# A planner's price for GpSimd's weighting of head pairs, and a new ring layout for VectorE's pairs, in a fused attention and FP4 feed-forward kernel

## The reference

```
xn   = layernorm(x)
q, k, v = split(xn @ w_attn + b_attn)                # 16 heads of 8 features
scores  = q k^T * 8**-0.5 + mask                      # mask = -log(delta + 1) for a key delta > 0 after the query,
                                                      # 0 at delta = 0, -inf for earlier keys
attn = softmax(scores) v ; attn @ w_proj + b_proj
gate, up = fp4(xn) fp4(w_gate)^T, fp4(xn) fp4(w_up)^T # blocks of 16 quantized to 8 levels and back
ffn  = fp4(silu(gate) * up) fp4(w_down)^T
out  = x + attn branch + ffn branch
```

## Time and profile before

| | |
|---|---|
| median of 3 runs | 598.94 us (597.7 to 599.84) |
| the profiled execution | 599.36 us, its span 597.6 us |
| PE (TensorE matmul) busy | 562.5 us, 94% |
| DVE (VectorE) busy | 547.1 us, 92% |
| POOL (GpSimd) busy | 503.2 us, 84% |
| ACT (ScalarE) busy | 409.3 us, 68% |
| granted TensorE clock, mean | 0.997 of full speed |

### The profile page before, as it was taken

The page is one execution under the profiler, slowest core; times in us unless marked ns, Lnnn a source line. Parts: engine busy times, 40 slices in busy tenths (PEclk is TensorE's granted clock), DMA queues, the critical chain, the costliest instruction groups (busy, mean ns, idle before and its releaser), DMA issues.

```text
span 597.6 us, 11270 instructions
## 1 busy us (share of the span) xinstructions
PE 562.5 (94%) x3791; PEld 247.5 (41%) x3791; DVE 547.1 (92%) x1165; ACT 409.3 (68%) x868; POOL 503.2 (84%) x409
## 2 busy tenths in 40 slices
PE   5999999999899999999999999999999998999995
PEld 4677844544343434333333333342344343343322
DVE  5999989998999899999999999999998989999672
ACT  4668486675665567766776676767666767677793
POOL 7378888797998889798999989897988889798773
PEclk9999999999998999999999999999999999999999
DMA  7434344010000001000000000000000000000000
GB/s 203 103 104 113 110 99 108 2 74 8 1 3 1 2 1 60 39 1 2 1 1 1 20 1 2 1 2 2 1 2 19 2 0 2 2 0 2 2 2 18
DMA packets 14832, 16.66 MB, mean 28 GB/s; under 512 B 1639, under 2 KB 14216, under 8 KB 14360
## 3 DMA queue, kind: packets, MB, share of 16 engines
q1 hardware_dynamic: 14240, 15.70, 9.5%
q10 hardware_dynamic: 536, 0.26, 0.2%
HBM read 11.75 MB, written 4.01 MB: 26 GB/s over the span
## 4 chain that ended last, share of the span: by engine, by line
PE 53%; DVE 27%; issue 7%; ACT 7%; POOL 5%; POOLq 0%; ACTq 0%; DVEq 0%
PE psum L1467 14%; DVE mxp L1240 13%; PE psum L1425 13%; PE psum L1449 10%; DVE ring L1267 4%; PE psum L1310 3%; POOL ring L895 3%; PE psum L1381 2%; ACT ring L1049 2%; PE psum L1400 2%; PE psum L1428 2%; PE psum L1383 1%; PE psum L1452 1%; DVE psum L1222 1%; DVE xw L1218 1%
## 5 line engine op out<-in xcount | busy, mean ns | idle before, releaser
L895 POOL TENSOR_TENSOR ring<-ring,dist 128x1024 f32<-128x1024 f32 (+3 forms) x223 | 398.6, 1815 | 51.6 <-ACT ring L1049 50.8
L1240 DVE TENSOR_REDUCE mxp<-psum 128x1 f32<-128x512 f32 (+3 forms) x640 | 354.7, 598 | 16.6 <-PE psum L1425 13.9
L1049 ACT ACTIVATE ring<-psum 128x512 f32<-128x512 f32 (+3 forms) x446 | 221.8, 557 | 93.5 <-PE psum L1452 46.8
L1425 PE MATMUL psum<-kop,qop 96*128 96x512 bf16 (+3 forms) x640 | 198.4, 352 | 7.2 <-DVE mxp L1240 3.7
L1449 PE MATMUL psum<-qop,kop 128*128 128x512 bf16 (+3 forms) x640 | 191.2, 349 | 7.4 <-DVE mxp L1240 2.8
L1467 PE MATMUL psum<-ring,vaug 128*32 128x512 f32 (+3 forms) x1280 | 155.3, 556 | 2.5 <-POOL ring L895 1.9
L1267 DVE TENSOR_TENSOR ring<-psum,dist 128x512 f32<-128x512 f32 (+3 forms) x194 | 115.1, 620 | 12.0 <-ACT psum L1049 11.4
L1049 ACT ACTIVATE psum<-psum 128x512 f32<-128x512 f32 (+3 forms) x194 | 99.7, 545 | 31.7 <-PE psum L1449 19.0
L1425 PEld LDWEIGHTS psum<-kop,qop 96*128 96x128 bf16 x640 | 56.5, 97 | 134.6 <-DVE mxp L1240 45.5
L1449 PEld LDWEIGHTS psum<-qop,kop 128*128 128x128 bf16 x640 | 59.3, 97 | 83.6 <-DVE mxp L1240 19.7
L1428 PE MATMUL psum<-tri_q,identb 128*128 128x128 bf16 x256 | 55.9, 220 | 0.0
(11 more groups left out here) (134 smaller groups left out, 467.9 us busy)
## 6 DMA issues: line engine op xcount, KB each, us to landing
parts_dram<-qpart SPq DMA_DIRECT2D x18, 128.0 KB, 3.4
kop<-parts_dram SPq DMA_DIRECT2D x6, 384.0 KB
qop<-parts_dram SPq DMA_DIRECT2D x6, 384.0 KB
xin<-_attn_hidden_states_dram SPq DMA_DIRECT2D x4, 256.0 KB, 5.0
ring<-inv_dram SPq DMA_DIRECT2D x1, 1024.0 KB, 5.1
out_dram<-xin SPq DMA_DIRECT2D x4, 256.0 KB, 2.3
qop<-parts_dram SPq DMA_DIRECT2D x3, 288.0 KB
kop<-parts_dram SPq DMA_DIRECT2D x3, 288.0 KB
```

What stands on the lines that cost most here:

```text
L895: g_.tensor_tensor(slot(p)[:, 0:n], slot(p)[:, 0:n], both, ALU.mult).then_inc(weighed_pool, 1)
L1049: a_.activation(scores if pair_vec[p] else slot(p)[:, 0:n, e % 2], scores, ACT.Exp, scale=SCALE).then_inc(exp_done, 1)
L1240: v_.tensor_reduce(mxp[:, u % 2, 4 * a + j, c - g:c - g + 1], bank(*o)[:, 0:n], AX_X, ALU.max).then_inc(max_used, 1)
L1425: ins = mm(bank(*o)[:, 0:n], qop[0:K_MAX, u // NQ % 2, h, P * a:P * (a + 1)], kop[0:K_MAX, h, k0:k0 + n], start=True, stop=(c != g))
```

## The change

Two constants of the model are changed, and the layout of a slot of `ring` for VectorE's pairs.

- `POOL_COL, POOL_START` go from 2.04 ns and 220 ns to 1.906 ns and 140 ns. All engines' lists and the split of pairs are walked anew with them.
- A slot of a pair that VectorE weighs holds its two heads one behind the other, each 512 values without gaps; GpSimd's pairs stay interleaved. The helper `weighted(p, j, n)` gives a head's place to VectorE's write, ScalarE's write (for GpSimd's pairs only) and TensorE's read.

```
-POOL_COL, POOL_START = 2.04, 220
+POOL_COL, POOL_START = 1.906, 140
...
+        def weighted(p, j, n):
+
+            if pair_vec[p]:
+                return slot(p).rearrange("p n j -> p (n j)")[:, GQ * j:GQ * j + n]
+            return slot(p)[:, 0:n, j]
...
-                    a_.activation(scores if pair_vec[p] else slot(p)[:, 0:n, e % 2], scores,
+                    a_.activation(scores if pair_vec[p] else weighted(p, e % 2, n), scores,
...
-                    v_.tensor_tensor(slot(p)[:, 0:n, e % 2], bank("st", e)[:, 0:n], weights(d, n),
+                    v_.tensor_tensor(weighted(p, e % 2, n), bank("st", e)[:, 0:n], weights(d, n),
...
-                                 slot(2 * s + j // 2)[:, 0:n, j % 2], start=(b == NT - 1), stop=(b == TPG * g))
+                                 weighted(2 * s + j // 2, j % 2, n), start=(b == NT - 1), stop=(b == TPG * g))
```

## The result

The changed kernel takes 601.7 us (median of 7 runs, 601.04 to 602.95) against 599.61 for the kernel before in the same number of runs (597.7 to 601.27): ratio 1.0043, 95% interval 1.0025 to 1.0061. I had forecast 595.0 us and faster; it is slower by 0.43%, that is 2.6 us. The time lies within the stated range of 588 to 604, with the wrong sign.

The account below looks back on a forecast made before the run. VectorE, with TensorE, was taken as the late engine and GpSimd as the early one. 599.36 - 6.2 (VectorE relieved) + 2.1 (GpSimd loaded) = 595.3 us, less 0.42 for the median, forecast 595.0 us, range 588 to 604.

Parts of the forecast that it names:

- Price of a pair, and pairs moved: GpSimd's weighting: new price 2% too low by duration, 1% by cadence; 17 of VectorE's 97 pairs move, at most 21.
- What it is worth: Chain that ended last: 6.2 us off through VectorE, 2.1 us added by GpSimd, net gain 4.1 us.
- VectorE's relief: VectorE's weightings: 21 us less work, 3.8% off its 27% share of the chain, worth 6.2 us.
- GpSimd's added work: GpSimd's weightings: 36 us more work, 7% on its 5% share of the chain, costing 2.1 us.
- It fits, barely: Window 150 to 550 us: GpSimd's added 23 to 27 us fit into 36.5 us of waits for exponentials.
- waits for exponentials: Sign in the next profile: GpSimd's idle time for exponentials, 50.8 us over the whole span, falls below 25 us.
- GpSimd becomes late: Products at L1467 wait for GpSimd's pairs, 28 steps more, 9 us, giving 604 us; 0.32 together with an unlucky reshuffle.
- The reshuffle: All lists walked anew, places shift: no sure sign, 2 or 3 us either way; unlucky case within the 0.32.
- Layout: VectorE's contiguous writes and TensorE's reads of its pairs: costed at 0, at most 1 us gained.
- Last stretch: Last 37 us: GpSimd takes more pairs, ScalarE's 2.25 us step covers it; costed at 0, 1 us if cover fails.

Follow-up runs that it names:

- h4: Changed kernel with POOL_START 200 instead of 140, a full pair priced at 2152 ns, 89 pairs for VectorE: ratio 1.0105 to the kernel before.
- f3: Kernel before, lists kept, VectorE weighing only half of each head's columns from pair 64 on: ratio 0.9923 to the kernel before.
- f1: Kernel before, lists kept, GpSimd leaving out the last eighth of each pair's columns: ratio 1.0012 to the kernel before.
- f2: Changed kernel, lists kept, GpSimd leaving out the last eighth of each pair's columns: ratio 0.9923 to the kernel before.
- f4: Changed kernel, lists kept, VectorE weighing only half of each head's columns from pair 64 on: ratio 1.0043 to the kernel before.
- g4: Kernel before with POOL_START 222 instead of 220, 98 pairs for VectorE: 602.66 us, ratio 1.0049 to the kernel before.
- the six nudges: POOL_START moved by 1 or 2 ns, four times in the kernel before, twice in the changed kernel: ratios 1.0049 to 1.0112 to the kernel before.
- e1: Kernel before with only the new slot layout, old prices, so lists and split unchanged: ratio 1.0013 (0.9997 to 1.003) to the kernel before.
- h1: Walk at the old price, but the split read from a table, that of the changed kernel (84 for VectorE): 609.18 us, ratio 1.017.
- h2: Walk at the new price, but the split read from a table, that of the kernel before (97 for VectorE): 616.40 us, ratio 1.0296.
- g3: Kernel before with POOL_START 218 instead of 220, 98 pairs for VectorE: 604.70 us, ratio 1.0097 to the kernel before.
- e3: Kernel before with POOL_START 219 instead of 220, 102 pairs for VectorE: ratio 1.0112 to the kernel before.

## Why the prediction was wrong, by its own steps

**Price of a pair, and pairs moved.** Right in kind. I took 17 of a possible 21, and it was 13 in sum: VectorE lost 11.5 us instead of 21 (13 * 1.24 = 16 was to be had by my own price of a pair, and its weightings did lose 16.4), GpSimd gained 24 us instead of 36. The price itself I read a little wrong. I took 10.54 / 5 = 2.11 us as the cadence and called the new price 1% too low; but the last of a row is recorded in full, so the cadence in the earlier trace rows is (10.54 - 2.14) / 4 = 2.10 us, and in the changed kernel seven in a row give (14.71 - 2.14) / 6 = 2.095:

```profile
398.61 14.71 POOL L901 TENSOR_TENSOR ring<-ring,dist 128x1024 f32<-128x1024 f32 x7 [0.60 <-ACT ring L1055]
```

The new price of 2092 ns is right on it. A price below the truth was thus no reason for GpSimd's lateness, and h4, which raises it to 2152, didn't cure it.

**What it is worth: the step that failed.** I priced VectorE's relief by its share of the chain, "27% of 598", which made 6.2 us of 21, 0.30 us for each us of work. f3 measured 0.15. With the 11.5 us that moved it is 1.7 us, not 6.2. A share of the chain says where the chain runs, not what is saved when it is cut there: another chain of almost the same length is next, and in f3 it shows at once (VectorE falls to 10%, GpSimd rises to 12%). I priced GpSimd's added work the same way, by its 5% of the chain, 2.1 us. f1 shows no gain behind that 5% in the kernel before, f2 shows 0.15 us a us in the changed one; so 24 us more cost between 0 and 24 * 7.2 / 46.5 = 3.7 us. These two slopes give between -1.7 and +2.0 us, an estimate from f1 to f4, where I had -4.1. The measured +2.6 us (1.5 to 3.7) needs the upper end and something of the walk beside it.

**"It fits, barely".** By the sums it did fit: between 150 and 550 us GpSimd's work grew by 14.6 us and its waits for exponentials fell from 36.5 to 21.4. But a fit of sums doesn't say that each pair comes out in time. GpSimd's pairs queue up without a pause from 423 to 448 us, and in the same window TensorE's products now wait 8.0 us for them. Over the whole span the waits for exponentials should have fallen below 25 us and are 33.0, with 24 us of added work in place of 36.

**The rival "GpSimd becomes late"** had the place and the size of the waits. It was to decide from 13 more waits at L1467 on. There are 16 more, worth 8.8 us, against the 9 us and 28 waits that I had written. Its time, 604 us, took each us of waiting for a us of the run, and that is wrong: g4 has 2 us more waits than the kernel before and loses 0.49%, the changed kernel has 8.8 us more and loses 0.43%. I gave the rival 0.32 together with a bad reshuffle. By the Trainium skill ("GPSIMD Engine Reference", Key points), VectorE is about twice as fast, and I had estimated 2.5 us for a pair from that; the trace has 2.1, and GpSimd turned late all the same.

**The reshuffle** was mis-sized. "2 or 3 us either way" from VectorE's 16 waits; the six nudges measured 0.49 to 1.12%, 3 to 7 us, all of them slower than the kernel before. I had reckoned with places in the lists only, but 113 of the 320 pairs change their engine for 13 in sum. No row of the profile prices this; but the kernel before should have been taken as one walk out of many, and any new walk as a draw without its luck.

**Layout.** Costed at 0 with -1 us as a bound, and e1's interval holds 0. (In the working of that bound 0.03 * 512 is 15 ns, not 13; the bound stays at 1 us.) Rows by shape of the changed kernel, against the earlier trace rows:

```profile
L1473 PE MATMUL psum<-ring,vaug 128*32 128x512 f32 x896 | 124.8, 621 | 10.1 <-POOL ring L901 9.1 <-DVE ring L1273 0.4 <-issue 0.2
L1273 DVE TENSOR_TENSOR ring<-psum,dist 128x512 f32<-128x512 f32 x120 | 78.6, 681 | 13.5 <-ACT psum L1055 13.0 <-PE psum L1473 0.4
```

681 ns with a contiguous write as with a strided one, and 621 for 623.

**Last stretch: the term that I put at 0.** Full steps still follow at ScalarE's pace, as costed: two products of the changed kernel, four steps apart, are (586.35 - 577.34) / 4 = 2.25 us from one to the next. But I gave the cover of ScalarE to all of the stretch, the short steps at its very end too, and there nothing hides GpSimd: the last exponential ends at 589.96 us, and GpSimd works until 591.19. Two pairs of 256 queries are 2 * 1.16 = 2.3 us on GpSimd in a row, and both went to it. That is 1.8 us of the 3.4 between the two spans, by the chain and by h1 and h2. The late fall of the clock, 0.9 us more, I had not seen coming.

**What stays open.** Why the neighbours at the old price lose 0.5 to 1.1% with nearly the same load is settled only in part: their spans are 5.3 us (g3), 5.0 (e3) and 3.3 (g4) longer than that of the kernel before; the last steps account for 1.9 us in g3 and e3, the late clock for 0.9 us in all three, and 2.2 to 2.5 us of each stay unexplained. Nor is it settled how the 0.43% divides between GpSimd's load and the new draw: both were measured, each alone is large enough, and h1 and h2 show that they don't add up. The changed kernel was not run with its last pairs given to VectorE and all else kept, which would have priced the last steps by themselves.

## What to carry to other kernels

When fixed lists come out of a greedy walk, nudge a constant by a nanosecond a few times before crediting any change of its constants: here that alone moved the time by up to 1.1%, more than the change under study, and a tuned kernel may be the lucky draw. Where three engines are busy for 84% of the span or more, price relief of one by a cut of its work with the lists kept, not by its share of the chain: here a us off the binding engine gave 0.15 us. Idle time that suffices for more work in sum doesn't say that the work will be done in time, and a more accurate price in the planner need not give a faster list. Look at the last two steps by themselves: what hides a slow engine in mid-run is gone there.

## What the runs showed of the hardware

At the end of this kernel TensorE can drop to half its clock: in the changed kernel it was busy 2.3 us of 5 with no gap over 1.24 us, and eight matmuls of 128 columns then ran in 2.04 us instead of 1.13; 15 filling transposes brought 1.16 back. GpSimd's product of two float32 operands, 1024 values a partition, takes 2.137 us by its mean record and 2.095 from start to start in a full queue, since records overlap; a price for a queue is taken from the cadence.
